# The set-up of a state-space mixer, moved into the program of its main loop and turned from token-major to head-major

## The reference, cut to what matters

```
h    = layernorm(x)
gate, hBC, dt = split(h @ in_proj_w.T)        # 8192, 8192 + 2*1024, 128
hBC  = silu(causal_conv4(hBC) + conv_b);  x, Bm, Cm = split(hBC)
dt   = softplus(dt + dt_bias)                  # one number per token and head
A_dt = -exp(A_log) * dt
cum  = cumsum(A_dt) within chunks of 128 tokens
Y_diag = ((C B^T) * exp(cum_l - cum_s), l >= s) @ (x * dt)
states = per chunk: (B * exp(cum_last - cum))^T @ (x * dt), carried with exp(cum_last)
Y_off  = (C @ carried state) * exp(cum)
y = rmsnorm(Y_diag + Y_off + D * x) * norm_w * silu(gate)
out = y @ out_proj_w.T
```

## Time and profile before

| what | value |
|---|---|
| time, median of 3 runs | 2315.89 us (2315.21 to 2316.35) |
| time of the profiled execution | 2316.08 us |
| its span, first to last instruction | 2314.4 us |
| PE busy | 2179.6 us, 94% of the span |
| DVE busy | 1647.3 us, 71% |
| ACT busy | 1387.7 us, 60% |
| POOL busy | 875.1 us, 38% |
| mean granted clock of TensorE | 0.971 of 2.4 GHz |

### The profile page before, as it was taken

How to read it: one execution, slowest core, us unless ns; L and a number is a source line. 1 busy time by engine, 2 the same in 40 slices (tenths; PEclk the granted TensorE clock), 3 DMA queues, 4 the chain that set the end, 5 groups by cost and what they waited for, 6 DMA issues and landing times. The chain is left out here.

```text
span 2314.4 us, 37238 instructions
## 1 busy us (share of the span) xinstructions
PE 2179.6 (94%) x13426; PEld 1781.1 (77%) x13426; DVE 1647.3 (71%) x2692; ACT 1387.7 (60%) x1856; POOL 875.1 (38%) x616
## 2 busy tenths in 40 slices
PE   4799975989999999999999999999999999959999
PEld 3588854778888888888888888888888888747887
DVE  5655553777877778787777878778787877755554
ACT  1222221777777777777777777777777777712221
POOL 0122210444444444444445444444544444402221
PEclk9899985999999999999999999999999999969999
DMA  2443311333223333333323323333333323234431
GB/s 77 164 163 117 128 43 64 106 94 106 104 93 104 93 109 97 104 104 93 104 95 112 99 98 104 93 104 98 108 103 94 104 93 105 74 124 158 163 125 75
DMA packets 128210, 242.72 MB, mean 105 GB/s; under 512 B 13104, under 2 KB 47792, under 8 KB 127792
## 3 DMA queue, kind: packets, MB, share of 16 engines
q1 hardware_dynamic: 128048, 240.58, 32.1%
HBM read 234.23 MB, written 6.29 MB: 104 GB/s over the span
## 5 line engine op out<-in xcount | busy, mean ns | idle before, releaser
L816 PE MATMUL ring<-m_lnt,w_sb 128*128 128x512 f32 x3456 | 867.7, 400 | 22.4 <-POOL w_sb L1157 17.8
L816 PEld LDWEIGHTS ring<-m_lnt,w_sb 128*128 128x128 f32 x3456 | 639.6, 189 | 166.6 <-POOL w_sb L1157 18.1
L1157 POOL TENSOR_TENSOR w_sb<-w_raw,w_sb 128x512 fp32r<-128x512 f32 x288 | 429.4, 1495 | 384.0 <-ACT w_sb L925 379.7
L1034 DVE SCALAR_TENSOR_TENSOR xc<-ring,cw,xc 128x511 f32<-128x511 f32 (+2 forms) x384 | 287.4, 748 | 186.4 <-ACT xc L937 177.3
L893 PE MATMUL ring<-wo,ygs 128*128 128x512 f32 x1536 | 387.8, 401 | 2.5 <-POOL wo L1162 2.5
L1169 POOL TENSOR_TENSOR ysq<-ysq,y 128x512 f32<-128x512 f32 x128 | 165.0, 1289 | 527.4 <-ACT y L969 527.4
L893 PEld LDWEIGHTS ring<-wo,ygs 128*128 128x128 f32 x1536 | 282.6, 189 | 64.0 <-issue 3.1
L925 ACT ACTIVATE w_sb<-w_raw 128x512 fp32r<-128x512 f32 x288 | 177.7, 623 | 48.0 <-DMA w_raw<-w_in 48.0
L360 POOL TENSOR_TENSOR f_gu<-f_gu_f,f_gu 128x1024 fp32r<-128x1024 f32 x28 | 67.2, 2401 | 358.0 <-ACT f_gu L385 358.0
L937 ACT ACTIVATE xc<-ring,cb,cw 128x512 f32<-128x512 f32 x128 | 99.2, 775 | 165.5 <-PE ring L816 165.5
L874 PE MATMUL yt<-em,x_dt 128*64 128x128 f32 x2048 | 183.6, 279 | 1.0 <-DVE em L1091 1.0
(11 more groups left out here) (157 smaller groups left out, 3130.2 us busy)
## 6 DMA issues: line engine op xcount, KB each, us to landing
w_raw<-w_in SPq DMA_DIRECT2D x288, 256.0 KB, 4.3
ce<-e_t SPq DMA_DIRECT2D x128, 384.0 KB, 4.2
wo_raw<-w_out SPq DMA_DIRECT2D x128, 256.0 KB, 4.5
f_gu_q<-gu_w SPq DMA_DIRECT2D x28, 512.0 KB, 5.1
f_gu_zr<-gu_z SPq DMA_DIRECT2D x28, 512.0 KB, 5.9
f_gu_sr<-gu_s SPq DMA_DIRECT2D x28, 512.0 KB, 7.3
f_dn_q<-dn_w SPq DMA_DIRECT2D x28, 256.0 KB, 6.8
f_dn_zr<-dn_z SPq DMA_DIRECT2D x28, 256.0 KB, 7.1
```

Of the source, the lines that this page charges most:

```text
L816: mm = nc.tensor.matmul(dst[:], w_sb[:, u % WR, wp, k * P:(k + 1) * P], lnt[:, xp, k, b * S:(b + 1) * S], start=(i == 0), stop=(i == 3 * K ...
L1034: nc.vector.scalar_tensor_tensor(out=dst[:, d:S], in0=src[:, 0:S - d], scalar=cw[:, tile, j:j + 1], in1=dst[:, d:S], op0=ALU.mult, op1=ALU ...
L1157: nc.gpsimd.tensor_tensor(w_sb[:, u % WR, 1], w_raw[:, u % NR], w_sb[:, u % WR, 0].bitcast(F32), ALU.subtract).then_inc(w_lo, 1)
```

## The change

What it does, in the order of the run:

- In f1, after each of the last 8 residual additions DVE takes the mixer's statistics of that tile. SP issues eight loads ahead of the stores of x: the mixer's constants, the weight of dt, and the first two units (b and c).
- Prologue and main block are one block. The statistics' second half, the square root, the normalisation and its turn stand at its head, now with four buffers for `xn` and six PSUM banks.
- dt is projected with heads as output rows and 512 tokens as columns, 24 matmuls in place of 96. Softplus, cum and the decays are made in that layout. dt and the decays are turned back by PE (`turn_dt`, `turn_dec`) and copied to `dt_q` and `dec_q`. exp of the chunk's last cum is spread over the partitions by a product with ones (`spread_last`).
- ACT makes the bf16 parts; there are three and no negated copies: `a_right` holds -1 in place of 1 in its fill rows, and `a_left` reads the same three parts. DVE makes the two remainders.
- POOL fills `a_left` and `a_right`, makes the low part of dt's weight, a diagonal tile for `spread_last` and the product `dec_h`. The zero fills of `ysq` and `acc` are gone: the first addition to each is a copy.
- The prologue's work stands between the projections of units b, c, x and z and now also x of the second pair, which was projected at the start of step 0.

The core of the diff (declarations are left out):

```diff
+        def load_early(sp):            # in f1, ahead of the stores of x
+            sp.dma_start(cw[:], conv_w).then_inc(m_w, 16)
...
+            sp.dma_start(wdt_raw[:], w_in[DT_T]).then_inc(m_w, 16)
+            sp.dma_start(w_raw[:, 0], w_in[B_T]).then_inc(w_loaded[0], 16)
+            sp.dma_start(w_raw[:, 1], w_in[C_T]).then_inc(w_loaded[1], 16)
+        def mixer_stats(t):            # in f1, behind residual t, behind a wait for it
+            nc.vector.bn_stats(m_stats[:, t], xr[:, t]).then_inc(m_stats_done, 1)
# SP, main block
+                sp.dma_start(a_neg[:], a_log.to_broadcast([P, H])).then_inc(a_in, 16)
                 load_units(-1)
+                load_units(0)
+                for i in range(3):
+                    if i == 2:
+                        sp.wait_ge(cum_exp, 3)
+                        sp.dma_start(e_t, e_cum[:]).then_inc(scratch_stored, 16)
+                    sp.wait_ge(parts_done, i + 1)
+                    sp.dma_start(a_parts[i], parts[:, i]).then_inc(scratch_stored, 16)
+                sp.wait_ge(scratch_stored, 16 * 4)
                 load_args(0)
-                load_units(0)
# PE
+                for t in range(6):
+                    turn_norm(t)
+                project_dt(0)          # waits for 4 low parts and wdt's low part
+                turn_norm(6)
+                turn_norm(7)
+                project_dt(1)
+                project(("b", 0))
+                project(("c", 0))
+                project(("x", 0))
+                turn_dt()              # waits dt_done
+                project(("z", 0))
+                cumulate()             # 2 x 4 matmuls of 128 columns
+                project(("x", 1))
                 gram(0)
+                spread_last()          # 2 matmuls of 512 columns
+                turn_dec()             # 2 x 4 transposes through one bank
# ACT
+                nc.scalar.activation(wdt[:, 0], wdt_raw[:], ACT.Copy)
+                nc.scalar.activation(m_rstd[:], m_rstd[:], ACT.Sqrt)
+                w_high(("b", 0))
+                for t in range(T):
+                    norm_high(t)
+                    if t == 1:
+                        w_high(("c", 0))
+                nc.scalar.activation(a_neg[:], a_neg[:], ACT.Exp)
+                w_high(("x", 0))
+                nc.scalar.activation(low[:], low[:], ACT.Exp)
+                nc.scalar.activation(low[:], low[:], ACT.Ln, bias=1.0)
                 tap(("b", 0))
+                w_high(("z", 0))
                 tap(("c", 0))
+                w_high(("x", 1))
                 tap(("x", 0))
+                ... cum <- ARG, twice, ACT.Copy
+                ... parts[:, 0] <- cum, ACT.Copy
+                ... e_end <- Exp of 8 columns;  diff <- Exp(diff)
+                ... parts[:, 1] <- rest, ACT.Copy   # waits rest_done 1
+                ... e_cum <- Exp(cum)
+                ... parts[:, 2] <- rest, ACT.Copy   # waits rest_done 2
+                tap(("x", 1))
+                w_high(("z", 1))
                 activate_z(0)
                 activate_bc(0)
                 activate_x(0)
                 copy_btok(0)
+                ... e_last <- ST, YT, ACT.Copy, twice
# DVE
+                for t in range(T):     # tensor_scalar L113's form, then norm_low(t - 2)
+                ... pre <- ARG + dtb_col, twice;  low <- min(-pre, pre)
                 conv(("b", 0))
+                ... dt_h <- max(pre, 0) + low       # both inputs in SBUF
+                ... a_dt <- XT, ST times a_neg;  dt_q <- XT, ST
                 conv(("c", 0))
+                ... diff <- cum_last - cum
                 conv(("x", 0))
+                ... rest <- cum - parts[:, 0]       # both in SBUF
+                ... rest <- rest - parts[:, 1]      # both in SBUF
                 mask_gram(0)
+                ... dec_q <- XT, once a batch
# POOL
+                ... memset a_left, a_right, then 1.0 and -1.0 into 3 rows, four times
+                ... wdt low part
+                w_low of b0, c0, x0, z0, x1
+                ... pre <- ident * e_end, 128 x 1024   # waits cum_exp 1, dt_done
+                ... dec_h <- diff * dt_h, 128 x 1024
+                w_low(("z", 1))
# the parts and the accumulators
-                    sp.dma_start(a_left[32:35, k % 2], a_parts[3:6, h:h + 2, b * S:(b + 1) * S])
+                    sp.dma_start(a_left[32:35, k % 2], a_parts[0:3, h:h + 2, b * S:(b + 1) * S])
+                    if HALF * i % JP == 0:
+                        nc.vector.tensor_copy(acc[:, at], ring_bank(("out", (i, t)))[:])
+                    if pair(k) == 0:
+                        nc.gpsimd.tensor_copy(part, y[:, k % 2])
```

More of the change, by code:

```diff
@@ new lines, in cumulate, with spread_last @@
+                def cumulate():
+                    for b in range(B):
+                        pe.wait_ge(adt_done, b + 1)
+                        for c in range(CPB):
+                            mm = nc.tensor.matmul(ARG[:, b, c * CS:(c + 1) * CS], a_dt[:, b, c * H:(c + 1) * H], tri[:],
+                                                  start=True, stop=True)
+                        mm.then_inc(cum_mm, 1)
+                def spread_last():
+                    pe.wait_ge(diag_done, 1)
+                    pe.wait_ge(adt_done, 2 * B)
+                    for b in range(B):
+                        nc.tensor.matmul((ST, YT)[b][:], ones[:],
+                                         pre[:, b * S:(b + 1) * S],
+                                         start=True, stop=True).then_inc(last_mm, 1)
@@ new lines, in turn_dec @@
+                def turn_dec():
+                    pe.wait_ge(dec_done, 1)
+                    for b in range(B):
+                        need(pe, decq_done, b)
+                        for c in range(CPB):
+                            at = b * S + c * CS
+                            mm = nc.tensor.transpose(XT[:, c * H:(c + 1) * H], dec_h[:, at:at + CS],
+                                                     ident[:])
+                        mm.then_inc(dect_mm, 1)
+                for t in range(6):
+                    turn_norm(t)
@@ L986, in _ @@
+                w_high(("x", 0))
+                act.wait_ge(pre_done, B + 1)
+                nc.scalar.activation(low[:], low[:], ACT.Exp).then_inc(softplus, 1)
+                act.wait_ge(softplus, 2)
+                nc.scalar.activation(low[:], low[:], ACT.Ln, bias=1.0).then_inc(softplus, 1)
                 tap(("b", 0))
+                w_high(("z", 0))
                 tap(("c", 0))
+                w_high(("x", 1))
                 tap(("x", 0))
+                for b in range(B):
+                    act.wait_ge(cum_mm, b + 1)
+                    nc.scalar.activation(cum[:, b * CPB:(b + 1) * CPB].rearrange("p c l -> p (c l)"), ARG[:, b], ACT.Copy)                        .then_inc(cum_done, 1)
@@ new lines, in _ @@
+                act.wait_ge(cum_done, B)
+                nc.scalar.activation(parts[:, 0], cum[:].rearrange("p c l -> p (c l)"), ACT.Copy).then_inc(parts_done, 1)
+                nc.scalar.activation(e_end[:], cum[:, :, CS - 1], ACT.Exp).then_inc(cum_exp, 1)
+                act.wait_ge(diff_done, 1)
+                nc.scalar.activation(diff[:], diff[:], ACT.Exp).then_inc(cum_exp, 1)
+                act.wait_ge(rest_done, 1)
+                nc.scalar.activation(parts[:, 1], rest[:], ACT.Copy).then_inc(parts_done, 1)
@@ L989, in _ @@
+                nc.scalar.activation(e_cum[:], cum[:].rearrange("p c l -> p (c l)"), ACT.Exp).then_inc(cum_exp, 1)
+                act.wait_ge(rest_done, 2)
+                nc.scalar.activation(parts[:, 2], rest[:], ACT.Copy).then_inc(parts_done, 1)
+                tap(("x", 1))
+                w_high(("z", 1))
                 activate_z(0)
-                for unit in units_of(0):
-                    w_high(unit)
                 activate_bc(0)
@@ L994, in _ @@
                 copy_btok(0)
+                for b in range(B):
+                    act.wait_ge(last_mm, b + 1)
+                    nc.scalar.activation(e_last[:, b * CPB:(b + 1) * CPB].rearrange("p c h -> p (c h)"), (ST, YT)[b][:],
+                                         ACT.Copy).then_inc(last_done, 1)
                 for k in range(STEPS):
@@ L1226, in build @@
         scope_m.close()
+        early.close()
         ffn("f2", acc, out)
```

379 lines of the change are left out of this document (194 added, 185 removed).

## The result

| | before | after |
|---|---|---|
| time, median (lowest to highest) | 2316.12 us (2315.21 to 2316.96) | 2273.39 us (2271.88 to 2275.19), 4 runs |
| ratio, with 95% interval | 1 | 0.9816 (0.9804 to 0.9828) |
| profiled execution, and its span | 2316.08 us, 2314.4 us | 2275.19 us, 2273.5 us |

The change saves 42.7 us by the medians and 40.9 us by the two profiled executions. The sign was right, the size was not. They come from where the buffers lie in SBUF, the memory from which the engines read their operands.

The account below looks back on a forecast made before the run. PE bounds the main loop; before it, one chain of engines waiting on each other sets the time. Terms 3.9 + 17.0 - 3.0 - 0.9 + 17.0 = 34.0 us saved, 2316.1 to 2282.1 us; range 2275 to 2290.

Parts of the forecast that it names:

- The time from there to the end unchanged: Sign to look for: from z of step 0 to the kernel's end nothing changes; wrong if the loop's 1500 us differ by over 2.
- Nothing done in the main loop on another engine can pay there: Main loop and most of both feed-forward layers: PE busy 1498.0 of 1500 us, so other engines' work there gains nothing.
- Start of the block: Block's start to first normalisation: statistics move into f1, off the chain; saves 3.9 us.
- Normalisation and dt's projection: First normalisation to the end of dt's projection: 24 matmuls, clock rising 4.2 us in; saves 17.0 us.
- Softplus to dt: End of dt's projection to dt: `conv` of b and a DVE meeting with POOL delay dt; costs 3.0 us.
- dt to the third part: From dt to the third bf16 part: ACT's chain, with both remainders meeting POOL's work; costs 0.9 us.
- Third part to z of step 0: Third bf16 part to z's projection in step 0: most work there is done earlier; saves 17.0 us.
- 1, the clock stays low: Rival: half clock in both halves of dt's projection and through z of step 0; saving 28.5, 2287.6 us; chance 0.13.
- 2, no meetings and a better clock: Rival: POOL's work misses DVE's, `gram` and `spread_last` run at full clock; 2276 us; chance 0.10.
- 3, the drain: Rival: each ACT table switch in the set-up costs a 1.38 us drain beside its load; 2285 us; 0.10 with the late feeder.
- 4, a late feeder: Rival: POOL's three-row fills cost twice 0.9 us, so dt's weight comes 1 us late; 2283; chance 0.10 with the drain.
- 5, the loop locks into another phase: Rival: DVE-POOL meetings hold PE up in each of 128 loop steps; at 0.8 us each, 2350 us; chance 0.04.

Follow-up runs that it names:

- e6: The kernel before with only its buffers placed where the changed kernel has them, no instruction altered: 2305.77 us, ratio 0.9958.
- b1: Separate kernel computing nothing of the reference: PE alone runs 512-column matmul streams at varied operand distances; intervals 226.7 to 234.2 ns.
- e8: The changed kernel with the mixer's eight statistics moved from f1 back to the main block's head: 2280.55 us, ratio 0.9847.
- e3: The changed kernel with `conv` of x1 moved from behind `decay_c` to ahead of `mask_gram` on DVE: 2272.30 us, ratio 0.9811.
- e4: The changed kernel with POOL's diagonal tile and `dec_h` held until DVE has made both remainders: 2273.70 us, ratio 0.9815.
- e7: The changed kernel with the edits of e3 and e4, and buffers placed for operand distances at multiples of 256 bytes: 2262.64 us, ratio 0.9770.

## Why the prediction was wrong, point by point

**The step that failed.** "The time from there to the end unchanged", and "PE's order from step 1 on is the old one" behind it. The second half-sentence is true. The inference is not: the same order does not give the same time if the buffers move. The diff moved `w_sb`, `w_raw` and `wo` into other scopes, and with them the distance between the two operands of 4992 matmuls. The prediction put the loop at nothing; the missing term is -10.3 us (e6, medians), and with it the sum would have been 2271.8, 1.6 from the median. That nearness is partly luck, since the set-up's terms were 3.6 too high (30.4 for 34.0), and 1.6 us of the loop and 1.7 behind it go with the clock. For the program alone, from e6 to the kernel after, the forecast of 34.0 stands against 32.4. The text did name the sign by which it would be known, the loop's 1500 us differing by more than 2.

**"Nothing done in the main loop on another engine can pay there".** True of other engines; PE's own matmuls could go faster, and a busy share of 1498 in 1500 us had been read as a limit. (Rows 1 show this for the loop; for the feed-forward layers, of which the sentence says the same, they show nothing.) The row shows that PE was never idle, not that its matmuls came as fast as they can: 232.7 ns where b1 shows 226.7.

**Start of the block, 3.9 us.** Right, and shown by e8.

**Normalisation and dt's projection, 17.0.** 16.4. The rise of the clock was forecast at 4.2 us into the first half; it came about 4 us into it, and the second half ran at full clock (3.07 us). The reading behind the forecast was loose: by the shares of the earlier trace rows, 0.78 and 0.81, the two rises came at about 380.9 and 404.8, 6.1 us after L615 had begun at 374.77 (4.3 after L617 at 376.63) and 4.6 after L816, not 4.2 to 5.6. That the rise was met within 0.2 us is luck: in e3 the clock was back before the first half began, in e4 1.6 us into it, and the work up to there is the same. The first half began 1.75 us after its forecast place, 1.3 of which is the block's own late start.

**Softplus to dt, -3.0.** -2.9, with `conv` of b and the meeting where they were forecast. POOL's L1230 ends at 353.84 + 2.52 = 356.36, and 356.36 + 1.23 - 0.1 = 357.49; dt was ready at 357.44.

**dt to the third part, -0.9.** -1.2, with both further meetings. For the last one POOL ends at 373.28, plus 1.23 less 0.1 is 374.41, and DVE ended at 374.36. e4 shows the cause of the two longer remainders by its removal. The Trainium skill (SBUF — State Buffer, Who interferes with whom, with the section on its two sides) says that a DVE operation with two SBUF inputs and a GpSimd one that reads SBUF hold the port for a whole instruction, and the loser blocks fully. These rows agree.

**Third part to z of step 0, 17.0.** 14.3. The mis-sized term: DVE's work behind `dec_q` was put down as "behind z". But z of step 0 takes over the ring bank of x1, which `conv` of x1 has to free, and `conv` stood behind `decay_c`. The wait is 3.44 us, and `decay_c` (2.02 here, 0.95 in most steps) met POOL as a fourth meeting that was not counted. Without the wait the term would have been 17.7. e3 removes it, and with it the term is 31.1 - 13.4 = 17.7. The ring's order had been called "the old one from step 0's z on", which is so; what freed the bank was not followed.

**The rivals.** 1, the clock stays low: wrong for dt's second half, right for z of step 0, which took 4.42 us instead of 3.0. 2, no meetings and a better clock: neither. It has nearly the measured time, 2276, and for a wrong reason. 3, the drain: the logarithm's table load started 0.02 us after the exponential's end (349.14 + 1.06 = 350.20, 350.22), took 1.28, and the logarithm followed 0.01 behind. A drain would show as a gap or a longer load, and the 1.38 us that the Trainium skill states (ScalarE: Activation LUTs, What ACT_TABLE_LOAD costs) are in neither. 4, a late feeder: a fill of 3 rows cost 0.94 to 1.11 us, near the 0.9 taken; no operation waited for it. 5, the loop locks into another phase: it was the one that looked at the loop, and expected it only to get worse. Its sum is wrong: 128 steps at 0.8 us are 102 us, which with 2282 gives 2384 and not 2350. Nor was all that DVE has to spare proof against it: e8 shows one step and e7 five in which a meeting holds PE up by 1.1 to 1.3 us.

## What to carry to other kernels

Where a diff moves an allocation, compare the addresses of the operands of the most frequent matmuls in both kernels, and not only the order of the work: 32 bytes were worth 12 us of 2273 here by medians. A busy share near 100% says that an engine never idles, not that its instructions come as fast as they can; look at the interval of their starts. And where work is moved ahead, follow each buffer to be reused to the operation that frees it, and ask what stands ahead of that one on its engine.

## What was not expected of the hardware

- The start-to-start interval of 512-column matmuls of this 32-bit kind, with a weight load for each, depends on the distance between the two operands in SBUF (start of the weights less start of the columns), with a period of 256 bytes: 226.7 to 227.5 ns at 0, 229.0 at 192, 232.5 at 128, 233.2 to 234.2 at 32, 64 and 96 (b1, at full clock).
- A wait of PE for DVE appeared in the loop when PE's matmuls came 1.3% closer together: 7.1 us against 1.3 between 500 and 1900 us, and 7.3 in e6, where nothing but the placement differs from the kernel before.
- Which of two operations of DVE and POOL starts first, by 0.02 to 0.12 us, decided the length of a whole step: 16.40 us with POOL first (e8), 15.13 with DVE first (the kernel after).
- POOL's fill of 3 rows of 1024 bf16 took 0.94 to 1.11 us, as long as that of 128 rows of 1024 32-bit numbers (0.96).
